# Moving the third batch's key projection from the beginning into the first body

## The reference, cut to what matters

```python
q = split_heads(layernorm(x) @ Wq.T + bq)     # (16, 64, 128)
k = split_heads(ctx @ Wk.T + bk)              # ctx (16, 1601, 128)
v = split_heads(ctx @ Wv.T + bv)
weights = softmax(q @ k.T / sqrt(8))          # 16 heads, 64 x 1601
x = x + (weights @ v) @ Wo.T + bo
```

## Time and profile before

| | us |
|---|---|
| median of three executions | 585.04 |
| profiled execution | 585.52 |
| its span | 583.7 |
| PE busy | 526.1 |
| DVE busy | 418.8 |
| ACT busy | 380.7 |
| POOL busy | 323.8 |

### The profile page before, as it was taken

How to read it: one execution, slowest core, us unless ns; L and a number is a source line. 1 busy time by engine, 2 the same in 40 slices (tenths; PEclk the granted TensorE clock), 3 DMA queues, 4 the chain that set the end, 5 groups by cost and what they waited for, 6 DMA issues and landing times. The chain is left out here.

```text
span 583.7 us, 18814 instructions
## 1 busy us (share of the span) xinstructions
PE 526.1 (90%) x7882; PEld 341.0 (58%) x7882; DVE 418.8 (72%) x749; ACT 380.7 (65%) x704; POOL 323.8 (55%) x197
## 2 busy tenths in 40 slices
PE   2887999999998897999999898999889888999997
PEld 1634555665565464655655565665457565777776
DVE  6187888798797695887887887735887578555554
ACT  4874667677678575776777776976582616656562
POOL 1697968558558456576577279602200024676673
PEclk9887999999999998999999998999999979999999
DMA  7898664674574571754752946101100000000001
GB/s 214 127 131 132 140 104 91 97 117 89 86 116 89 87 108 39 117 105 71 123 106 35 144 84 110 40 2 53 47 2 2 2 1 1 2 2 0 0 0 37
DMA packets 16425, 41.62 MB, mean 71 GB/s; under 512 B 4006, under 2 KB 6830, under 8 KB 16234
## 3 DMA queue, kind: packets, MB, share of 16 engines
q1 hardware_dynamic: 15608, 40.09, 39.6%
q10 hardware_dynamic: 740, 0.42, 0.2%
HBM read 19.70 MB, written 0.52 MB: 35 GB/s over the span
## 5 line engine op out<-in xcount | busy, mean ns | idle before, releaser
L899 DVE TENSOR_REDUCE half_max<-wide 128x2 f32<-128x802 f32 x256 | 241.8, 988 | 57.5 <-PE wide L584 53.6
L824 ACT ACTIVATE probs<-score 128x512 f32<-128x512 f32 (+1 forms) x416 | 225.8, 596 | 75.4 <-PE score L635 75.0
L655 PE MATMUL sums<-probs,values 128*32 128x192 f32 (+3 forms) x3328 | 134.7, 282 | 5.9 <-issue 5.9
L655 PEld LDWEIGHTS sums<-probs,values 128*32 128x32 f32 (+1 forms) x3328 | 87.8, 110 | 60.0 <-issue 31.6
L584 PE MATMUL wide<-k_stack,q_cur 48*128 48x401 bf16 x512 | 88.9, 343 | 13.3 <-ACT k_full L806 6.2
L635 PE MATMUL score<-q_cur,k_stack 50*128 50x128 bf16 (+1 forms) x1664 | 83.4, 219 | 9.6 <-ACT probs L824 5.0
L415 POOL TENSOR_TENSOR ctx_hi<-ctx_in,one 128x1601 bf16<-128x1601 f32 x15 | 42.9, 2860 | 77.3 <-PE wide L506 68.5
L635 PEld LDWEIGHTS score<-q_cur,k_stack 50*128 50x128 bf16 (+1 forms) x1664 | 52.3, 95 | 35.0 <-ACT probs L824 11.3
L1892 POOL TENSOR_TENSOR hid_lo<-hid_e,hid_hi 114x512 bf16<-114x512 f32 x47 | 54.2, 1158 | 32.7 <-ACT hid_hi L1916 31.4
L427 POOL TENSOR_TENSOR k_hi<-k_full,one 128x1601 bf16<-128x1601 f32 x15 | 42.9, 2857 | 43.2 <-ACT k_full L806 34.7
L2027 DVE SCALAR_TENSOR_TENSOR hid_e<-gu,keep_bgu,gate 114x512 f32<-114x512 f32 x48 | 35.9, 750 | 38.5 <-ACT gate L1929 38.3
(11 more groups left out here) (327 smaller groups left out, 923.7 us busy)
## 6 DMA issues: line engine op xcount, KB each, us to landing
k_stack<-k_hi SPq DMA_DIRECT2D x64, 204.0 KB, 6.5
ctx_in<-in_ctx SPq DMA_DIRECT2D x56, 200.1 KB, 3.2
k_stack<-k_lo SPq DMA_DIRECT2D x32, 204.0 KB, 8.7
ctx_in<-in_wgu SPq DMA_DIRECT2D x16, 171.0 KB, 4.9
keep_w<-in_w SPq DMA_DIRECT2D x1, 1368.0 KB
ctx_in<-in_ctx SPq DMA_DIRECT2D x1, 800.5 KB, 8.3
keep_x<-in_x SPq DMA_DIRECT2D x1, 512.0 KB, 6.9
q_cur<-shift SPq DMA_DIRECT2D x30, 2.0 KB
```

The costliest lines, as they stand in the source:

```text
L655: last = pe.matmul(sums[32 * g:32 * g + 32, first * LQ:(first + heads) * LQ], values[0:m, n, k, VW * g + 2 * c:VW * g + 2 * c + 32], probs ...
L824: nc.scalar.activation(probs[0:m, step % NPROB, :].rearrange("r (g p c) -> r p g c", g=G, p=2)[:, p], score[0:m, (2 * step + p) % NSCORE, ...
L899: dve.tensor_reduce(half_max[:, b % 2, :, u // 4, u % 4], wide[:, w, :].rearrange("p (c k) -> p c k", c=2)[:, :, 0:CH], AX.X, ALU.max).the ...
```

## The change: what it does

The two key halves of batch 2 leave the beginning and become ring entries of body 0 at steps 1 and 3. Those of batch 3 stay at steps 9 and 11. The four spare entries go. POOL splits the context of batch 3 in the place where it split the keys of batch 2, and those keys behind it. `vals(2, 0)` has a wait of its own for `s_split` of batch 2, which it had through the keys before.

```diff
 def keys_at(i, k):
 
-    steps = K_STEPS if i else (9, 11)
-    return [(i + PREFETCH, steps.index(k))] if k in steps and i + PREFETCH < B else []
+    if i == 0:
+        return [{1: (2, 0), 3: (2, 1), 9: (3, 0), 11: (3, 1)}[k]] if k in (1, 3, 9, 11) else []
+    return [(i + PREFETCH, K_STEPS.index(k))] if k in K_STEPS and i + PREFETCH < B else []
...
-               ("v", 1, 3), ("q", 2, 2), ("q", 2, 3)] + [("k", 2, c) for c in range(4)]
+               ("v", 1, 3), ("q", 2, 2), ("q", 2, 3)]
...
             def split(b):
...
-                    made = [RING["v", b - 2, 1]] + ([RING["k", b - 2, 1]] if b > 4 else [])
-                    if b == 4:
-                        spare_made(pool, ("k", 2, 3))
+                    made = [RING["v", b - 2, 1], RING["k", b - 2, 1]]
                     pool.wait_ge(s_wide, 1 + max(made))
...
             def split_keys(b):
-                if b < PREFETCH:
+                if b == 1:
                     spare_emptied(pool, ("k", b, 3))
                 else:
                     is_empty(pool, ("k", b, 1))
...
             for what in LATE_Q[0:G]:
                 low_queries(what)
+            split(3)
+            lay_queries(2)
             split_keys(2)
-            lay_queries(2)
-            split(3)
             for what in LATE_Q[G:]:
                 low_queries(what)
...
             def vals(b, half):
                 n, w = b % 2, half_free(pe, ("v", b, half))
+                if b == 2 and half == 0:
+                    pe.wait_ge(s_split, b)
...
                 maxima(0, u)
                 if u < 10:
                     make_spare(SPARE_LATER[u])
-                elif u >= 12:
-                    make_spare(SPARE_LATER[u - 2])
```

## The result

The changed kernel took 594.12 us, the median of four executions (589.73 to 596.45), against 584.48 for the kernel before (582.83 to 585.71). The ratio is 1.0128, 95% interval 1.0071 to 1.0186, which is 7.5 us on 584.48. On a second chip, with more executions: 592.93 against 584.50, ratio 1.0134 (1.0081 to 1.0186). The median of the first four lies 0.6 us above the forecast's range, the ratio (592.0 us) and the second chip's median lie in it. So it is slower, as forecast, by half as much again as the 5.2 us that were forecast. The ratios leave out executions more than 1.5% above the fastest of their kernel (among them one of 653.95 us in run 2, four of twelve in run 7 and three of twelve in run 10), while the medians keep them, so that the two can differ.

A forecast was written before the change was run, and what follows sets the result against it. PE's list was taken to set the pace, with DVE setting it in body 0's steps 0 to 7. Terms +4.5, +0.9 and -0.3 gave +5.1 us on 585.52, 590.6, or 590.2 as median; range 586.5 to 593.5.

The forecast's parts named there:

- The beginning: Before body 0: without key chunks units end 2.8 us earlier, shift and clock cost 0.2, body 0 starts at 49.2.
- The halves: Body 0, steps 1 and 3: the halves cost 1.6 us of DVE's time (0 to 2.1), mostly hidden in PE's wait.
- more on top: Rival: the wait comes plus earlier half clock in body 0 (+2), shift behind loads (+1.3), more half clock (+0.5); about 594; chance 0.14.
- The stack: Batch 2's stack lands at 74.3, 15.05 us after ACT's end; PE waits 5.4 us, unit 0 is 4.5 us late.
- After the wait: Between batch 2's unit 0 and body 1's scores: half clock costs 0.9 us, ready exponentials may give back 0.3.
- The rule that I read from the earlier trace: PE's clock: a 1.21 us stop drops it to half; full returns only after 2.82 us of unbroken work.
- SP's queue: SP's loads move behind the stack; batch 1's shift lands about 80.5, needed at 81: costs 0, at most 1.5 us.
- in time: Rival: faster stack DMAs or a later step 10 let the stack come in time; 584.0, or 582.4 with free halves; chance 0.08.
- absorbed later: Rival: slack in body 1 gives back 2 to 4 us; 586 to 588 for half, under 586.8 for all; chance 0.12.

The follow-up runs named there:

- run 2: The changed kernel with batch 2's key halves at steps 0 and 1 of body 0 instead of 1 and 3; 588.15 us, ratio 1.0074.
- run 7: The kernel before with 11 unread matmuls on PE before its wait for `ctx_lo` at unit 12; 591.40 us, ratio 1.0083.
- run 10: The changed kernel with batch 2's maxima from step 0 of body 1, later weights and half of batch 5's context issued behind batch 1's shift; 589.93 us, 1.0049.
- run 4: The kernel before with batch 2's maxima from step 0 of body 1 instead of step 10 of body 0; 588.28 us, ratio 1.0055.
- run 6: The kernel before with batch 2's four key chunks left out of the beginning and put nowhere; 584.50 us against 584.00, ratio 1.0038.
- run 8: The changed kernel, halves at steps 0 and 1, unread matmuls behind units 12 to 15 of batch 0 and before batch 2's unit 0; 592.82 us, 1.0152.
- run 11: The changed kernel with key halves at steps 0 and 1 and batch 2's maxima from step 11 of body 0; 587.41 us against 585.93, 1.0010.
- run 12: The changed kernel with batch 2's maxima over batch 1's stack, later weights and half of batch 5's context issued behind batch 1's shift; 590.80 us, 1.0117.
- run 5: The changed kernel with 50 unread matmuls on PE right before its wait for batch 2's stack; 593.23 us, ratio 1.0178.
- run 3: The changed kernel with batch 2's maxima from step 0 of body 1 instead of step 10 of body 0; 596.34 us, ratio 1.0188.
- run 9: The changed kernel with batch 2's maxima taken over batch 1's stack, so PE doesn't wait at unit 0; 594.20 us, ratio 1.0151.

## Why the prediction was right, and where its sizes were off

*The beginning.* Its step said 44.15 for the last unit and 49.2 for body 0; it was 43.74 and 49.56, with PE held 0.50 us by the shift, whose transfer took 4.0 us instead of 3.0; the prediction had bounded its lateness at 0 to 2.3 us. Runs 4 and 6 to 8 show that this transfer, not PE, is the floor there: scores at 49.3 to 51.2, with PE waiting 1.4 to 2.6 us for it. The prediction took the clock of the beginning for a property of the program. Run 4 shows that it is not, so the 2.2 us, near the 2.6 that were said, are in part the luck of the execution that was profiled.

*The halves.* DVE gaps of 0.67 and 1.06 stand where 0.6 and 1.2 were said. The half clock of 57.86 to 61.06 is not there; the prediction's rival *more on top* had it come earlier, and of the profiles of kernels with the halves in body 0 two have it: run 8 (49.9 to 53.2) and run 10 (51.8 to 61.8), where it costs the 3.5 us told there. Step 10's scores are at 68.77, 0.87 earlier than before; the step said 1.0. Runs 2, 11 and 12 agree that they are not the loss.

*The stack.* The mechanism is as forecast, wait, place and chain. From ACT's end (59.48) to unit 0 it was 15.82 us, where the step took 15.05 from batch 3. `k_lo` went out 6.29 us after ACT's end (6.31 for batch 3 before). The 0.8 is in the landing, which I took from the first DMA's issue although the view's 8.9 is the longest of two whose second is issued 0.6 later. ACT was done 0.2 later than said. So unit 0 was 5.4 us late instead of 4.5.

*After the wait.* This is the term that was mis-sized: 0.9 less 0.3 stood for what measured 1.83 (7.80 against 5.97). I had let the half clock last 2.8 us into the stretch, from a stretch of values; it lasted until 80.8, 5.5 us, with PE busy nearly all the while. Run 5 shows that the 1.8 is the clock. The rule that I read from the earlier trace rows does not hold either way: run 4 has the stop of 1.21 us without half clock, run 11 a stop of 1.00 us with it, and after the wait full clock came back in 3.6 us there, 6.9 in run 2, 13.3 in run 3. The two measured terms, 5.42 and 1.83, are the 7.25 us by which body 1 is late; the ratio gives 7.5, with an interval of 4.2 to 10.9.

*SP's queue.* The step said that the shift of batch 1 would arrive when needed and cost 0. In the changed kernel it does (issued at 78.97, and body 1 waits for ACT at 83.10). What I had not seen is that it does so only because PE is late. When PE's wait is put off or taken away, in runs 3 and 9, a wait of 6 to 7.5 us for the shift takes its place, and in run 12 one for the next stack. The cause is one: before, the DMA engines moved stack and weights in 52 to 67 and were nearly idle until batch 3's stack; now the same bytes start 12 us later (62.45 against 50.63), and everything behind them in the queue is late by turns. The rival "in time" would therefore not have given 584.0 by a later step 10, since its wait goes over to the shift (run 3, 596.34). For faster DMAs, its other condition, no run shows what it would have given.

*The rival "absorbed later"*: the profiled executions differ by 4.2 us at the end, 7.25 at body 1. The turn of batch 8 comes 2.3 us later than before, after 7.8 at batch 5. This is no slack of the changed kernel. The execution of before that was profiled lost time in bodies 6 and 7 to stops as in runs 5 and 7, 2.00 us at 198.10 and this one:

```profile
221.59 0.50 PE L635 MATMUL score<-q_cur,k_stack 50*128 50x128 bf16 x6 [2.67 <-issue]
```

What stays open is why the totals of runs 5, 7 and 8 are worse by several us than their bodies 0 and 1. (For runs 3 and 10 a part is seen: half clock goes on to 94.1 and 92.7.) In each profile PE has stops of 1 to 3 us with no releaser, at other places when PE's program has other instructions; that they are what the fillers cost was not tested.

## What to carry to other kernels

When a step is moved to a later place, follow its product to the first reader through every queue, and compare that chain's length with the distance left; here 9.7 us were left (from ACT's end at 59.48 to step 10's place for the unit at 69.2) for a chain of 15.8. Then ask what stands behind it in the same queue: a transfer of 2 KB issued after 2.85 MB (stack 1.22, weights 1.23, half a context 0.40) landed 9.4 us later, with 1.63 MB of that taken from ahead of it 4.6 us later, and taking one wait away brings the next until the queue itself is relieved. A stop of PE can also cost the clock behind it, here another 1.8 us on 6.1. And before a clock is read from one profile as what a program does, a second profile of the same program should be looked at.

## What the runs showed of the hardware

TensorE's clock, in the profiles of runs whose PE waited in body 0 or at body 1: behind waits of 1.00 us (run 11), 1.96 (run 10), 2.56 (run 2), 6.14 (changed kernel), 6.19 (run 9) and 7.51 (run 3) the granted clock was 0.50, for 3 to 13 us of work. Where unread matmuls had filled the wait to within 0.55 and 0.42 us (runs 5 and 8), it stayed at 1.00. In the beginning one and the same program ran 41 to 47 us at half clock in one execution (the kernel before) and at full clock in another (run 4).

PE stops with no releaser recur. In the profiled execution of the kernel before those over 0.8 us are at 176.5, 198.1, 221.6, 335.6 and 357.3, spaced like bodies (21.6 to 23.5 us), and in the changed one, behind body 0, at 162.8, 225.3, 337.7 and 359.3. With 11 more matmuls at 39.7 us (run 7) they are at 133.0, 155.0, 177.7, 201.9, 226.6, 338.1 and 360.0. In the windows just ahead of several of them (195 to 196 and 218 to 219 us of before, 114 to 115 of run 5) the DMA view has one packet of 16 KB of the instruction queue. The execution of before has 59 packets of this queue (0.97 MB) and five such stops, so most packets have no stop behind them. That the stops are PE waiting for its instructions is a guess from this; no run tests it.
